# First attention layer of a four-layer graph network on one core: where the first masked product, the scaling of the last tiles and the copies of turned rows stand in the order

## What is computed

```python
# x here is _layernorm(x)
y = jnp.linalg.norm(x, axis=-1, keepdims=True)
A = x @ x.T / (y @ y.T)
A = A * b
A = jnp.tanh(A / 8.0) * 8.0
A = jnp.exp(A) * A_shape          # A_shape is adj
A = A / jnp.sum(A, axis=-1, keepdims=True)
x = A @ x
return x @ W.T + bias
```

## Time and profile before

| | |
|---|---|
| median of three runs | 886.03 us |
| span of the profiled execution | 869.3 us |
| runs' median less the span | 16.7 us |
| PE busy | 743.8 us (86%) |
| DVE busy | 661.3 us (76%) |
| ACT busy | 484.1 us (56%) |
| POOL busy | 273.4 us (31%) |

### The profile page before, as it was taken

How to read it: one execution, slowest core, us unless ns; L and a number is a source line. 1 busy time by engine, 2 the same in 40 slices (tenths; PEclk the granted TensorE clock), 3 DMA queues, 4 the chain that set the end, 5 groups by cost and what they waited for, 6 DMA issues and landing times.

```text
span 869.3 us, 15803 instructions
## 1 busy us (share of the span) xinstructions
PE 743.8 (86%) x5226; PEld 536.3 (62%) x5226; DVE 661.3 (76%) x2281; ACT 484.1 (56%) x723; POOL 273.4 (31%) x584
## 2 busy tenths in 40 slices
PE   3999999768999878999999987878778797798894
PEld 2455555427999634677778676655446675786563
DVE  6658686843444377899872699999898999999757
ACT  5777676414555326555563484668686675822153
POOL 3401412335666400211200052041341577770000
PEclk9999999997999899999999999788988898989897
DMA  8674100055888500000000000000000001101001
GB/s 149 104 119 67 38 7 20 26 158 163 236 231 235 156 14 0 2 1 2 2 1 1 2 2 2 2 1 2 1 0 2 2 1 56 43 2 32 1 1 49
DMA packets 47368, 41.95 MB, mean 48 GB/s; under 512 B 7376, under 2 KB 44112, under 8 KB 47280
## 3 DMA queue, kind: packets, MB, share of 16 engines
q1 hardware_dynamic: 29488, 19.95, 8.3%
q0 software_dynamic: 11456, 14.62, 8.2%
q10 hardware_dynamic: 6336, 6.32, 2.9%
HBM read 39.69 MB, written 9.57 MB: 57 GB/s over the span
## 4 chain that ended last, share of the span: by engine, by line
DVE 20%; PE 17%; issue 15%; POOLq 4%; ACT 4%; POOL 3%; DVEq 0%; ACTq 0%
PE bank L2148 4%; DVE big L1605 4%; PE bank L2131 3%; PE bank L2052 3%; DVE cand L1523 2%; DVE cand L1369 2%; DVE hacc L1518 2%; PE bank L2332 2%; PE bank L2345 1%; ACT big L1878 1%; DVE rm L1363 1%; ACT big L1848 1%; PE bank L295 1%; POOLq L1238 1%; DVE cand L1544 1%
## 5 line engine op out<-in xcount | busy, mean ns | idle before, releaser
L2131 PE MATMUL bank<-ident,big 128*128 128x128 f32 x512 | 81.5, 309 | 27.1 <-DVEq L1628 18.6
L1878 ACT ACTIVATE big<-bank 128x512 f32<-128x512 f32 x128 | 71.0, 597 | 49.9 <-PE bank L2131 48.7
L2131 PEld LDWEIGHTS bank<-ident,big 128*128 128x128 f32 x512 | 62.5, 156 | 54.8 <-ACT big L1878 20.4
L2052 PE MATMUL bank<-kk,qq 64*128 64x512 f32 x256 | 76.0, 710 | 17.0 <-ACT big L1848 16.4
L1848 ACT ACTIVATE big<-bank,negm 128x2048 f32<-128x2048 f32 x32 | 62.6, 1958 | 46.0 <-DVE fsc L1655 35.7
L2059 PEld LDWEIGHTS bank<-parts,adjT 128*128 128x128 bf16 x1536 | 86.6, 98 | 2.4 <-issue 2.1
L2059 PE MATMUL bank<-parts,adjT 128*128 128x128 bf16 x1536 | 87.9, 219 | 0.0
L1605 DVE SCALAR_TENSOR_TENSOR big<-big,st 128x2048 f32<-128x2048 f32 x32 | 73.9, 2347 | 3.3 <-PE bank L2131 3.3
L403 POOL DMA_INDIRECT ys_scratch<-big,parts x62 | 59.9, 967 | 32.6 <-ACT big L758 22.8
L848 PE MATMUL bank<-big,xn 128*128 128x512 f32 x128 | 62.2, 608 | 5.7 <-DVE big L550 5.7
L832 PE MATMUL bank<-xnT 128*128 128x512 f32 x128 | 62.4, 612 | 2.3 <-DVE xnT L539 2.3
(11 more groups left out here) (382 smaller groups left out, 1549.5 us busy)
## 6 DMA issues: line engine op xcount, KB each, us to landing
big<-in_L_ffn_w_dram SPq DMA_DIRECT2D x93, 128.0 KB
big<-in_adj_dram POOLq DMA_DIRECT2D x8, 512.0 KB, 7.6
big<-xs_scratch ACTq DMA_DIRECT2D x31, 132.0 KB, 2.9
kk<-in_adj_dram POOLq DMA_DIRECT2D x4, 512.0 KB, 8.2
qq<-in_adj_dram POOLq DMA_DIRECT2D x4, 512.0 KB, 10.0
xs_scratch<-hacc SPq DMA_DIRECT2D x9, 132.0 KB
xs_scratch<-hacc ACTq DMA_DIRECT2D x8, 132.0 KB
res<-in_x_dram SPq DMA_DIRECT2D x4, 256.0 KB, 6.9
```

The source lines that it names most:

```text
L1878: nc.scalar.activation(MT[:, 4 * q:4 * q + 4, s * P:(s + 1) * P], bank[:, 5 + q % 2, :].rearrange("p (j i) -> p j i", j=4), ACT.Copy).then ...
L2052: nc.tensor.matmul(bank[:, c, :], qq[lo:lo + DA, (g * G + s) * P:(g * G + s + 1) * P], kk[lo:lo + DA, c * CH:(c + 1) * CH], start=True, st ...
L2131: mm = nc.tensor.transpose(bank[:, 5 + q % 2, j * P:(j + 1) * P], mk[:, s, jt * P:(jt + 1) * P], ident[:, :])
```

## The change

On DVE the scaling of tiles is taken out of `norms` and becomes `unit(c)`, one quarter a call. Both calls of `norms` now come with less scaling between them and the loop: quarters 0, 1 and 2 are scaled ahead of the loop, quarter 3 behind the masked product of pass 0. The copies of quarters 2 and 3 out of bank 5 stand behind the masked products of passes 0 and 1. The copy of quarter 1 moves to ACT, at the end of its pass 0, and the three groups of `xn` that stood in ACT's passes 0, 1 and 2 stand in passes 1, 2 and 3. In PE's program the calls of `turn_wn(2)` and `turn_wn(3)` are written inside the loop.

```diff
-                    for t in tiles:
+
+                def unit(c):
+
+                    for t in range(c * TPC, (c + 1) * TPC):
                         nc.vector.tensor_scalar(wn[:, t, :], res[:, t, :], mean[:, t:t + 1], y2[:, 1, t:t + 1],
                                                 ALU.subtract, ALU.mult).then_inc(wn_ready, 1)
...
                 norms(range(0, TPC))
+                unit(0)
                 norms(range(TPC, NT))
+                unit(1)
+                unit(2)
...
-                take_wnT(1)
-                take_wnT(2)
                 for q in range(NQ):
...
-                    if q == 1:
-                        take_wnT(3)
+                    if q == 0:
+                        unit(3)
+                    if q < 2:
+                        take_wnT(2 + q)
                     if q:
                         add((q - 1) // NP, (q - 1) % NP)
...
-                act.wait_ge(wnT_done, 1)
-                nc.scalar.activation(xnT[:, 0:CH], bank[:, 5, :], ACT.Copy).then_inc(wnT_out, 1)
+                def take_wnT(c):
+
+                    act.wait_ge(wnT_done, c + 1)
+                    nc.scalar.activation(xnT[:, c * CH:(c + 1) * CH], bank[:, 5, :], ACT.Copy).then_inc(wnT_out, 1)
+
+                take_wnT(0)
...
-                    if q in (0, 1, 2):
-                        xn_of(range((q + 1) * TPC, (q + 2) * TPC), 2)
+                    if q == 0:
+                        take_wnT(1)
+                    if q in (1, 2, 3):
+                        xn_of(range(q * TPC, (q + 1) * TPC), 2)
...
                 score(2)
-                turn_wn(2)
                 for q in range(NQ):
                     c, p = divmod(q, NP)
-                    if q == 1:
-                        turn_wn(3)
+                    if q < 2:
+                        turn_wn(2 + q)
```

## The result

The changed kernel takes 883.18 us (median of 13 runs), the kernel before 886.05 (median of 13). The ratio is 0.9961, with a 95% interval of 0.9945 to 0.9976: 3.5 us less, between 2.1 and 4.9 (the medians alone differ by 2.9). The forecast was 881.5, and 4.5 us less.

The account below looks back on a forecast made before the run. PE was taken to bound the kernel from the first gather on, but not at the start. The terms 1.6 + 1.6 + 1.6 - 0.3 gave 4.5 us less, forecast 881.5 us, range 879.6 to 884.6.

Parts of the forecast that it names:

- Copy on ACT, 1.6 us: Start of layer A: quarter 1 copied on ACT, ending at 19.15, lets score(2) start at 19.2 instead of 20.8 us.
- first and the third term: Start of layer A: the copy of quarter 1 on ACT and the earlier first masked product on DVE, 1.6 us each.
- Clock, 1.6 us: At score(2): less PE idle time keeps the granted clock up, so it takes 1.71 instead of 3.28 us.
- first rival: At score(2): the clock falls all the same, gather(0) at 23.4, 3.2 us of gain, 882.8 us; chance 0.15.
- First masked product, 1.6 us: Ahead of gather(0): DVE's product runs 19.0 to 20.2, so turn_adj(2) to gather(0) takes 0.45 instead of 2.08 us.
- xn one pass later: ACT, early passes of layer A: 4.8 us of work in three passes; cover shrinks from about 1.8 to 1.2 us.
- rival of ACT as the bound: Three passes run at ACT's 4.8 instead of 4.0 us, 2.4 to 2.7 us back, 884.0 us; chance 0.14.
- DVE beside POOL, 0.3 us: Passes 4 and 5: DVE work beside POOL's adds makes gather(5) wait 0.3 us, until 42.5; bounds nothing and 1.3 us.
- Each DVE instruction waits out a whole add: Passes 4 and 5: 1.74 us of waiting per DVE instruction, gather(5) at 43.8, 3.2 us of gain, 882.8; chance 0.07.
- third rival: Beside POOL's adds, each DVE instruction waits a whole add of 1.74 us; gather(5) at 43.8, 882.8 us; chance 0.07.
- Behind 42 us nothing is lost: Behind gather(5): PE keeps the bound, the rest is chained to it, no load or table waits for a fixed time.
- slower rival: Later layers: three half-clock stretches last longer, PE loses up to 3.4 us each, 10.2 in all, 891.7 us; chance 0.04.

Follow-up runs that it names:

- e1: Kernel before with only the ACT part: quarter 1 copied on ACT, xn one pass later, DVE's twelve scalings and quarter 2 copy left ahead; 867.8 us, ratio 0.9979.
- e4: Kernel before plus 18 unread fp32 transposes on PE between turning quarter 1 and score(2); 884.26 us against 886.86, ratio 0.9979.
- after: First profiled execution of the changed kernel, against the kernel before; span 880.2 us, device time 881.92.
- ctrl_after: The changed kernel run again, on the same chip as the kernel before; 865.76 us against 869.37, ratio 0.9957.
- f1: The changed kernel run again, on a chip where the kernel before takes 868.62 us; 866.35 us, ratio 0.9971.
- e5: Changed kernel with ACT's xn back in passes 0 to 2, behind the copy of quarter 1; 882.24 us, ratio to the kernel before 0.9949.
- e3: Changed kernel with the table casts of DVE's pass 4 moved to pass 7; 882.74 us, ratio to the kernel before 0.9951.
- f3: Changed kernel with ACT's xn back in passes 0 to 2, run again on another chip; 863.65 us, ratio to the kernel before 0.9926.
- ctrl_before: The kernel before, unchanged, run and profiled again on a faster chip; 869.21 us, span 868.4.

## Why the prediction was right

The time lies in the range and gather(0) came where it was forecast, by the mechanism that was forecast. The sum was 1 us too large for the time, and parts of it were off in opposite directions.

*The bound.* PE was the bound from the first gather on, as read. Beside the waits named, PE's timeline is that of before, moved.

*Copy on ACT, 1.6 us.* Confirmed: score(2) 1.73 us earlier in the profile, 1.6 in e1. But its worth as a part was overrated: the DVE part alone brings score(2) forward to 19.2 and 19.8 in two profiles, since eight scalings end a microsecond sooner than twelve. The first and the third term share a cause, and the order on DVE alone carries nearly all of it.

*Clock, 1.6 us.* Nearly right in size (3.28 to 1.82 us, and e4), not in being settled. Of the six profiles with the copy on ACT and no added transposes, not counting e1, the clock stayed up in four (after, ctrl_after, f1, e5) and fell in two (e3, f3); e5 and f3 are the same kernel. In e1 it stayed. So forecast and first rival are both right, each for some executions. A median lies between them. From score(2) to gather(0) PE takes 4.4 us in e3 and f3 and 2.7 in f1, so a fall costs 1.7, and at two in six some 0.6 on the mean, an estimate from six profiles.

*First masked product, 1.6 us.* Confirmed: no idle time ahead of gather(0); in e1, without this part, the wait of 1.47 us remains.

*xn one pass later.* Its cover on ACT held: PE waited for no tanh and no adjacency copy. The rival of ACT as the bound is out.

*DVE beside POOL, 0.3 us.* Gather(5) waited 0.62, and two errors nearly cancelled. Product 4 was taken at 2.29 us; it met an add that was half done, took 1.64, and ended at 37.36 instead of 38.0. The copy and casts of pass 4 were taken at about 1 us and took 2.1 (39.50 to 41.63): the first cast stood behind the last add, 1.04 instead of 0.16, and L570 took 0.49 instead of 0.18 while POOL issued a load. That the sum came within 0.4 us is luck.

*Each DVE instruction waits out a whole add.* The prediction read the earlier trace rows as speaking against this, because the delay of 1.06 is less than the mean add of 1.74. That reading was wrong. The mean holds POOL's own waits; an add alone takes 1.27, and the rows after show each engine's instruction ending behind the other's, in turn. By that rule, which was the third rival's, a DVE instruction that comes early in an add waits about 1.1 us and one that comes late in it less, and that is also what the forecast had used for product 4 and the running sum. Forecast and third rival were one mechanism. The rival failed by its price of 1.74, charged to product 4 and to the running sum; gather(5) stood at 42.92, not at 43.8.

*Behind 42 us nothing is lost.* Here a step failed. The prediction had the rest chained to PE without loss. The lead at gather(5) was 4.1, 4.6 and 3.9 us (after, ctrl_after, f1), at the last gather the same within 0.1, and then 0.2 to 1.5 went with the falling clock ahead of the ranks. Further back the lead moves both ways; at the end ctrl_after and f1 have 4.0 and 3.4. The slower rival named this mechanism for the later layers and priced it at 10 us; nothing near that was seen.

*What lacks.* An estimate from the profiles: 3.9 us at gather(5) with scalings that begin at the same time as before's, less 0.6 for executions whose clock falls over score(2), less 0.5 behind layer A, is 2.8. The three comparisons gave 2.5 to 3.7. The prediction's own sign of being wrong, gather(5) at 42.5 and the time not moved by 3 us, is close to the comparison of f1 (43.08, 2.5 us).

*The chances.* The probabilities written down for faster, same and slower (0.74, 0.21, 0.05) don't follow from the list above them, which gives 0.78, 0.18 and 0.04.

*The absolute time.* The 16.7 us between span and runs were read as one thing: 1.7 lie around a span and the rest is between chips. It did no harm because the gain was taken off the median of runs.

## What to carry to other kernels

An engine's in-order queue is cheapest to fix where an early, short instruction stands behind work that nobody needs yet: four scalings and one copy moved behind the first product gave as much as the whole change, as far as the runs can tell. Moving work to another engine's idle time pays only if the work it displaces doesn't push a third engine's transfer or add into a worse place; look for whoever waits for the displaced work (here POOL, for xn). A gain that rests on the granted clock staying up is a gain in part of the executions: count it with its chance, or measure it over many. And where two engines take turns, the mean row of one holds its waits for the other: take the price of a wait from an instruction that ran alone.

## What the runs showed of the hardware

- The same kernel took 869 us on one chip and 886 on another, the difference lying in layer B: PE does 548 records from 200 to 290 us in ctrl_before and 476 in the profile after.
- A POOL add of two SBUF operands (1.27 us alone) and DVE products, sums and one cast between SBUF tiles took turns: each ended 1.08 to 1.13 us behind the other's end (the cast 0.03), though it had been started before it (after, 35.01 to 40.74; e3's product 5 took 2.09 by the last add). The cast of 128x16 numbers took 1.04 instead of 0.16. Small instructions suffer most, because the wait is what is left of the add, whatever their own length. A copy of 128x128 from a bank of PE's results took 0.28 beside an add (after) and without one (e5).
- With the same idle time of 0.69 us ahead of score(2), the granted clock stayed at 1.00 in ctrl_after, f1 and e5 and fell to 0.50 in e3 and f3. E5 and f3 are the same kernel, and f1, where it stayed, had idled longer ahead of the turning (0.88 us) than f3 (0.85), where it fell. Between executions of one order it differs.
- Two executions of the kernel before at the same pace stood 1.0 us apart one way at 684 us and 0.9 the other way at 848.
